# A macaron block on one core: the load queue written in block order, the scan's rows loaded twice, and z taken at the first place of a unit

## What is computed

```
x = x + 0.5 * ffn(layernorm(x))
x = x + attn(layernorm(x))
x = x + 0.5 * ffn(layernorm(x))

# attn: xz = x @ W_xproj.T -> delta_r (128), B (16), C (16)
delta = softplus(delta_r @ W_dt.T + b_dt)
dA = exp(delta * A);  Bu = delta * B * x          # 1024 channels x 16 states
h = dA * h + Bu                                   # over time
y = sum(h * C) + x * D_param
```

## Time and profile before

| | |
|---|---|
| median of 3 runs | 2799.12 us (2798.25 to 2800.99) |
| the profiled execution's own time | 2797.06 us |
| its span, first to last instruction | 2795.3 us |
| busy in the span | PE 2602.9, POOL 2348.2, DVE 2220.1, ACT 1496.2 us |
| mean granted PE clock | 0.985 |

### The profile page before, as it was taken

One profiled execution on the slowest core, in us unless ns is written; L12 is line 12 of the kernel. 1 busy time (PEld: TensorE's weight loads), 2 busy tenths in 40 slices (PEclk: granted clock), 3 DMA queues, 4 the chain that ended last, 5 costly groups with the idle time before them and its releaser, 6 DMA issues.

```text
span 2795.3 us, 39869 instructions
## 1 busy us (share of the span) xinstructions
PE 2602.9 (93%) x13664; PEld 1176.9 (42%) x13664; DVE 2220.1 (79%) x2933; ACT 1496.2 (54%) x3363; POOL 2348.2 (84%) x703
## 2 busy tenths in 40 slices
PE   4989999999999999999999999999999999989999
PEld 1444444444344443444444434444444443434444
DVE  8447888888888887888878888788888888888843
ACT  5346666665555655556555555565555554655521
POOL 2138889989899898998999989999899999989910
PEclk8999999999999999999999999999999999999999
DMA  5144544544354443644544445444455434454321
GB/s 219 48 116 137 144 127 131 161 142 139 109 164 140 135 138 112 163 140 127 147 143 132 144 137 163 138 126 129 151 153 158 143 119 141 136 145 145 91 58 53
DMA packets 303520, 373.50 MB, mean 134 GB/s; under 512 B 148435, under 2 KB 220243, under 8 KB 303318
## 3 DMA queue, kind: packets, MB, share of 16 engines
q1 hardware_dynamic: 286422, 337.40, 40.5%
q10 hardware_dynamic: 16896, 33.56, 4.1%
HBM read 234.05 MB, written 103.29 MB: 121 GB/s over the span
## 4 chain that ended last, share of the span: by engine, by line
PE 22%; DVE 19%; DVEq 5%; ACT 4%; DMA 4%; issue 4%; POOL 2%; SPq 1%; ACTq 1%; POOLq 0%
DVE mreg L1147 10%; PE pv L554 7%; PE po L554 5%; PE pv L558 3%; PE po L558 3%; PE py L721 2%; ACT pA L934 2%; DMA delta_scratch<-mreg 2%; DVE pv L1108 1%; DVE sel L1105 1%; DVEq L1113 1%; DMA mreg<-xnT_scratch 1%; DVEq L1107 1%; DVEq L1063 1%; DVE sel L1116 1%
## 5 line engine op out<-in xcount | busy, mean ns | idle before, releaser
L522 POOL TENSOR_TENSOR mreg<-mreg 128x2048 f32<-128x2048 f32 x256 | 1160.9, 4535 | 37.9 <-ACT hst L920 37.8
L1147 DVE TENSOR_TENSOR_SCAN mreg<-pA,hst,mreg 128x512 f32<-128x512 f32 (+1 forms) x1024 | 1042.9, 1065 | 98.9 <-ACT pA L934 70.0
L934 ACT ACTIVATE pA<-mreg,nA 128x512 f32<-128x512 f32 (+1 forms) x1280 | 739.0, 596 | 465.9 <-DVE mreg L1147 413.2
L512 POOL TENSOR_TENSOR mreg<-mreg 128x1024 f32<-128x1024 f32 x340 | 795.3, 2363 | 226.3 <-DMA mreg<-delta_scratch 219.6
L554 PE MATMUL pv<-wA,xT 128*128 128x512 f16 x2016 | 463.2, 382 | 40.5 <-DVE xT L1085 23.8
L554 PE MATMUL po<-wB,uT 128*128 128x512 f16 x2016 | 472.1, 381 | 13.5 <-DVE xin L1071 10.2
L554 PE MATMUL po<-wW,xT 128*128 128x512 f16 x2016 | 470.1, 380 | 0.0
L506 POOL TENSOR_TENSOR mreg<-mreg 128x2048 f32<-128x2048 f32 x86 | 389.7, 4532 | 1.4 <-issue 1.4
L554 PEld LDWEIGHTS pv<-wA,xT 128*128 128x128 f16 x2016 | 191.4, 98 | 323.1 <-ACT xT L841 60.3
L554 PEld LDWEIGHTS po<-wB,uT 128*128 128x128 f16 x2016 | 192.1, 98 | 277.9 <-issue 49.4
L554 PEld LDWEIGHTS po<-wW,xT 128*128 128x128 f16 x2016 | 196.0, 98 | 238.3 <-issue 24.6
(11 more groups left out here) (132 smaller groups left out, 2404.1 us busy)
## 6 DMA issues: line engine op xcount, KB each, us to landing
mreg<-delta_scratch SPq DMA_DIRECT2D x256, 512.0 KB, 6.0
delta_scratch<-mreg ACTq DMA_DIRECT2D x128, 256.0 KB
xin<-x SPq DMA_DIRECT2D x32, 512.0 KB, 3.7
x_scratch<-xin SPq DMA_DIRECT2D x32, 512.0 KB, 6.7
xnT_scratch<-auxs SPq DMA_DIRECT2D x32, 512.0 KB, 2.9
mreg<-xnT_scratch SPq DMA_DIRECT2D x64, 256.0 KB, 6.6
yT_scratch<-mreg SPq DMA_DIRECT2D x64, 256.0 KB, 2.5
uT<-yT_scratch SPq DMA_DIRECT2D x32, 512.0 KB, 4.7
```

Source lines behind the costliest of these rows:

```text
L512: pool.tensor_tensor(h[:, half * n:half * n + n, :], u, b.broadcast_to([P, n, c.width]), ALU.mult).then_inc(s_bm, 1)
L522: pool.tensor_tensor(h, h, by_c, ALU.mult).then_inc(s_cm, 1)
L934: last = nc.scalar.activation(dst[:, part, :], src[:, part, :], ACT.Exp, scale=nA[:, m:m + 1])
L1147: last = V.tensor_tensor_scan(h, split(pA[:, i % 2, :], c)[:, part, :], h, before, ALU.mult, ALU.add)
```

## The change

Four things change. **First**, SP's loads for the scan are no longer attached to groups (`slot`), but to blocks (`loads`): in each tile the first half of the next tile's inputs stands at place 6, the second at 7, the store of the tile before and the first delta pair at 9, the second delta pair at 15. A unit's blocks are listed in four parts: those of twentieths 0 to 2 at its head, 2 to 9 behind `turn`, 9 to 18 behind the stores of the rank rows, 18 to 20 behind the store of the unit's result. **Second**, a tile's rows of x are loaded twice: once for `delta` into one of two buffers that are free when `delta` has read them, and again at place 13 (`load_again`) into the third buffer, from which `sum_up` and the store work. **Third**, `plan` puts a tile's z at place 0 of the next unit that has none. A unit gets a second z, at place 1, only if the tile would otherwise come later than 10 groups before its own first group. **Fourth**, the load for the z at place 0 stands at the end of the unit before.

```
+AHEAD = 10
...
     for t in range(NTL):
-        s = 4 * t - 6
-        u, i = slot_unit[s] if s >= 0 else (SCAN0 - 1, 3)
-        at = (SCAN0 - 1, 2) if t == 0 else (u, 0) if i == 0 else (u, 1) if i < 3 else (u + 1, 0)
...
+        ready_at = f1_at[first_tile[t].row1 - 1] + 2 if t in first_tile else 0
+        late_u, late_i = slot_unit[max(4 * t - AHEAD, 0)]
+        at = (max(prev[0] + 1, ready_at), 0)
+        if at > (late_u + (late_i > 0), 0) and prev[1] == 0 and prev[0] >= ready_at:
+            at = (prev[0], 1)
...
             def load_tile(t):
                 sp.wait_ge(s_stn, 16 * chunk_of_tile[t].row1)
-                sp.wait_ge(s_sty[t % NXT], 16 * (t // NXT))
-                sp.dma_start(tile_of(t), blocks_of(xnT_u, t)).then_inc(s_ldt[t % NXT], 16)
+                sp.wait_ge(s_du, max(t - NXT + 2, 0))
+                slot = t % (NXT - 1)
+                sp.dma_start(tile_of(slot, t), blocks_of(xnT_u, t)).then_inc(s_ldt[slot], 16)
+
+            def load_again(t):
+                sp.wait_ge(s_sty, 16 * t)
+                sp.dma_start(tile_of(NXT - 1, t), blocks_of(xnT_u, t)).then_inc(s_ldv, 16)
...
-            def slot(a, n):
-                G = slot_of(a, n)
-                if G is None:
+            def loads(a, lo, hi):
+
+                if a.u < SCAN0 or a.u > SCAN1:
                     return
-                t = G // 4 + 1
-                if G % 4 == 2:
-                    if t >= 2:
-                        store_tile(t - 2)
-                    if t < NGRP // 4:
-                        spread_inputs(t, 0)
-                        spread_inputs(t, 1)
-                        spread_delta(t, 0)
-                if G % 4 == 3 and t < NGRP // 4:
-                    spread_delta(t, 1)
...
+                for i in range(block_at(a, lo), block_at(a, hi)):
+                    t, n = i // 16, i % 16
+                    if n == 6 and t + 1 < NTL:
+                        spread_inputs(t + 1, 0)
+                    if n == 7 and t + 1 < NTL:
+                        spread_inputs(t + 1, 1)
+                    if n == 9 and t >= 1:
+                        store_tile(t - 1)
+                    if n == 9 and t + 1 < NTL:
+                        spread_delta(t + 1, 0)
+                    if n == 13 and t < NTL:
+                        load_again(t)
+                    if n == 15 and t + 1 < NTL:
+                        spread_delta(t + 1, 1)
...
                 late = l if l and l.kind == 1 else None
-                if 0 not in a.zs:
-                    ranks_due(a, 1)
-                slot(a, 0)
-                if 0 in a.zs:
-                    load_tile(a.zs[0])
-                    ranks_due(a, 1)
+                ranks_due(a, 1)
+                loads(a, 0, 2)
...
                 turn(a, a.f2s + (b is not None and b.kind == 2))
-                slot(a, 1)
-                slot(a, 2)
                 if 1 in a.zs:
                     load_tile(a.zs[1])
+                loads(a, 2, 9)
...
-                slot(a, 3)
-                slot(a, 4)
-                if b:
-                    ranks_due(b, 0)
+                loads(a, 9, 18)
...
+                loads(a, 18, 20)
+                if b and 0 in b.zs:
+                    ranks_due(b, 0)
+                    load_tile(b.zs[0])
```

More of the change, by code:

```diff
@@ L95, in plan @@
     for t in range(NTL):
-        s = 4 * t - 6
-        u, i = slot_unit[s] if s >= 0 else (SCAN0 - 1, 3)
-        at = (SCAN0 - 1, 2) if t == 0 else (u, 0) if i == 0 else (u, 1) if i < 3 else (u + 1, 0)
[L99 to L102, removed]
+        ready_at = f1_at[first_tile[t].row1 - 1] + 2 if t in first_tile else 0
[3 more added lines that the diff above has]
+            at = (prev[0], 1)
+        if t == 0:
+            at = (SCAN0 - 1, 2)
+            assert f1_at[first_tile[0].row1 - 1] + 1 == at[0]
+        elif t > 2:
+            u, i = slot_unit[4 * t - 6]
+            assert at <= ((u, 0) if i == 0 else (u, 1) if i < 3 else (u + 1, 0)), (t, at)
         us[at[0]].zs[at[1]] = t
@@ L267, in build @@
         s_ldb = [sem(f"s_ldb{n}") for n in range(4)]; s_ldc = [sem(f"s_ldc{n}") for n in range(4)]
-        s_ldt = [sem(f"s_ldt{n}") for n in range(NXT)]; s_sty = [sem(f"s_sty{n}") for n in range(NXT)]
+        s_ldt = [sem(f"s_ldt{n}") for n in range(NXT - 1)]; s_ldv = sem("s_ldv"); s_sty = sem("s_sty")
         s_ldd = [sem(f"s_ldd{n}") for n in range(NPR)]; s_ldu = [sem(f"s_ldu{n}") for n in range(NPR)]
@@ L283, in column, with by_part @@
             return 16 * (channels_at(i // 16) + part) + i % 16
-        def rows_of(t):
-            return xt[:, t % NXT, :].rearrange("p (u k t) -> p k u t", k=chunk_of_tile[t].parts, t=P)
+        def by_part(slot, t):
+            return xt[:, slot, :].rearrange("p (u k t) -> p k u t", k=chunk_of_tile[t].parts, t=P)
         def split(a, c):
             return a.rearrange("p (k t) -> p k t", t=c.width)
-        def slot_of(a, n):
-            return a.slots[n] if n < len(a.slots) else None
         def block_at(a, twentieths):
@@ L331, in load_y @@
                     sp.wait_ge(s_out, a.u * 2 + 2)
-                    for n in range(NXT):
-                        sp.wait_ge(s_sty[n], 16 * len(range(n, chunk_of_row[b.v].tile1, NXT)))
+                    sp.wait_ge(s_sty, 16 * chunk_of_row[b.v].tile1)
                     src = yT_d[row:row + P, :].rearrange("p (k t) -> p k t", t=P)
@@ L382, in blocks_of, with tile_of @@
                 return d[:, c.row0:c.row1, k:k + c.parts, :].rearrange("p u k t -> p u (k t)")
-            def tile_of(t):
-                return xt[:, t % NXT, :].rearrange("p (u n) -> p u n", u=chunk_of_tile[t].rows)
+            def tile_of(slot, t):
+                return xt[:, slot, :].rearrange("p (u n) -> p u n", u=chunk_of_tile[t].rows)
             def load_tile(t):
                 sp.wait_ge(s_stn, 16 * chunk_of_tile[t].row1)
-                sp.wait_ge(s_sty[t % NXT], 16 * (t // NXT))
-                sp.dma_start(tile_of(t), blocks_of(xnT_u, t)).then_inc(s_ldt[t % NXT], 16)
+                sp.wait_ge(s_du, max(t - NXT + 2, 0))
[4 more added lines that the diff above has]
+                sp.dma_start(tile_of(NXT - 1, t), blocks_of(xnT_u, t)).then_inc(s_ldv, 16)
             def store_tile(t):
                 sp.wait_ge(s_y, t + 1)
-                sp.dma_start(blocks_of(yT_u, t), tile_of(t)).then_inc(s_sty[t % NXT], 16)
+                sp.dma_start(blocks_of(yT_u, t), tile_of(NXT - 1, t)).then_inc(s_sty, 16)
             def turn(a, y_done):
@@ L403, in turn @@
                     sp.dma_start_transpose(uT[:, part, :, :], src).then_inc(s_uc[part], 16)
-            def slot(a, n):
-                G = slot_of(a, n)
-                if G is None:
+            def loads(a, lo, hi):
+                if a.u < SCAN0 or a.u > SCAN1:
                     return
-                t = G // 4 + 1
-                if G % 4 == 2:
-                    if t >= 2:
-                        store_tile(t - 2)
-                    if t < NGRP // 4:
-                        spread_inputs(t, 0)
-                        spread_inputs(t, 1)
-                        spread_delta(t, 0)
-                if G % 4 == 3 and t < NGRP // 4:
-                    spread_delta(t, 1)
[L419 to L423, removed]
+                for i in range(block_at(a, lo), block_at(a, hi)):
[12 more added lines that the diff above has]
+                        spread_delta(t + 1, 1)
+                    for c in CH[1:]:
+                        if n % 4 == 0 and c.group0 - 4 <= i // 4 < c.group0:
+                            spread_b(c, i // 4 - c.group0 + 4)
+                        if n % 4 == 0 and c.group0 - 2 <= i // 4 < c.group0 + 2:
+                            spread_c(c, i // 4 - c.group0 + 2)
             def ranks_due(a, pos):
@@ L1129, in delta @@
                 dve.drain()
-                dve.wait_ge(s_ldt[t % NXT], 16 * (t // NXT + 1))
+                slot = t % (NXT - 1)
+                dve.wait_ge(s_ldt[slot], 16 * (t // (NXT - 1) + 1))
                 c = chunk_of_tile[t]
@@ L1133, in delta @@
                 V.tensor_tensor(dd[:, 1, :].rearrange(by_rows, k=c.parts, t=P), pz.rearrange(by_rows, k=c.parts, t=P),
-                                rows_of(t), ALU.mult).then_inc(s_du, 1)
+                                by_part(slot, t), ALU.mult).then_inc(s_du, 1)
             def scan(i):
@@ L1152, in sum_up @@
                 dve.wait_ge(s_e, 4 * t + 4)
+                dve.wait_ge(s_ldv, 16 * (t + 1))
                 c, k = chunk_of_tile[t], channels_at(t)
                 for n in range(c.parts):
-                    x_n = rows_of(t)[:, n, :, :]
+                    x_n = by_part(NXT - 1, t)[:, n, :, :]
                     y_n = split(py[:, :], c)[:, n, :].rearrange("p (u t) -> p u t", t=P)
```

## The result

The changed kernel takes **2819.5 us** (median of 4 runs, 2816.2 to 2822.1). The kernel before took 2800.05 us in the same comparison (2798.25 to 2803.07). The ratio is 1.007, with an interval of 1.0054 to 1.0086: slower by 0.7%, or 19.5 us, where 40 us less were forecast. The profiled execution took 2822.09 us, its span is 2820.3, and the mean granted clock is 0.982.

A forecast was written before the change was run, and what follows sets the result against it. PE and POOL were taken as nearly full, so what each waits for decides. Terms −73 − 7 + 37 + 3 = −40 us from 2797.06 gave 2757, forecast as 2760 us for the runs' median; range 2722 to 2798.

The forecast's parts named there:

- I take 0.65: Share of POOL's 112.3 us of input waits from `delta_scratch` expected to shorten the kernel: −73 us (bounds −30 and −112).
- length = POOL's work + POOL's idle: Ledger for stretches of eight units with the scan, such as 326.7 + 24.7 us; it set the gain's upper limit.
- comparison across rows 2: Units 24 to 31 against 40 to 47: 7.3 us more POOL idle, 9.5 us longer, so idle is paid in full.
- the waits change their names: Rival, chance 0.09: POOL waits for `hst` instead of inputs, only 0.27 of 112.3 us is won, 2802 us.
- So seven units at 5.3 us: Second delta pairs moved behind `turn` in units 10, 18, 26, 34, 42, 50, 58 come late: +37 us (+19 to +57).
- short stalls: Rival, chance 0.23: delta pairs land nearer 4 than 6.5 us, the seven cost 19 us, POOL's gain is 0.8; 2724 us.
- no slack between xn and PE: Unit 18: PE's `norm_blocks` started with no wait, so a late delta pair (5.7 us there) would delay PE.
- z at place 0: I take 0: 22 units move z ahead of the next unit's statistics; hidden by DVE's waits for PE, 0 us (31 us without cover).
- second z, −7: Units with two z: the earlier load of the tile's rows ends DVE's wait and PE's bank wait; −7 us (0 to −13).
- the second load at 0: 64 more loads of 256 KB for the tiles' rows, 16.8 MB, and their issues on SP: 0 us.
- The +3 for the ranks: Rank loads moved behind the result's store reach PE's z late ahead of unit 16: +3 us (0 to 5), once.
- the stalls outweigh: Rival, chance 0.13: late delta pairs hit units where PE had no wait; at 8.1 us each the sum is +23, 2822 us.

The follow-up runs named there:

- e9: e1 with both input halves moved from places 6 and 7 to place 9, behind the store of y: 2781.1 us.
- e1: The changed kernel with the second delta pair at place 12 instead of 15, for all tiles: 2759.1 us.
- e4: The kernel before with the double load of the rows and the new places of z, but the old queue by slots: 2781.1 us.
- e13: e1 with the place 0 z behind the next unit's statistics and norm on DVE and ACT, only in units with one z: 2740.9 us.
- e7: The changed kernel with the second delta pair at place 12 and z at the places of the kernel before: 2769.0 us.
- e3: The kernel before with only the double load of the tiles' rows added: 2798.5 us.
- e8: e1 with the second load of the rows at place 2 of the next tile instead of place 13: 2762.0 us.
- e6: The changed kernel with the second delta pair at place 12 only in units 10, 18, 26, 34, 42, 50 and 58: 2791.1 us.
- e15: The changed kernel with the second delta pair at place 15 only in units 10, 18, 26, 34, 42, 50 and 58, elsewhere at 12: 2789.2 us.

## Why the prediction was wrong

**"I take 0.65" of 112.3 us was the largest miss.** The waits ended, and with the pairs at place 12 that brought at most some 22 us (e9 to e1; e4 to e1, which is the whole of the queue's order, gives the same), not 73: a share of 0.2. The argument behind the share was the ledger "length = POOL's work + POOL's idle". It is true of any engine, bound or not, and so proves nothing about cause. The comparison across rows 2 (7.3 us more idle, 9.5 us longer) had the direction wrong: when another engine makes a unit longer, POOL's idle time grows with it. The kernel after shows it: its POOL is idle 198.5 us in units 3 to 59 against 174.7 before, without the input waits. The rival "the waits change their names" named the mechanism rightly, and its share of 0.27 was near. What decided was in the trace: PE waited for POOL 8.2 us in all, and for xn 36.7. That 8.2 is not the whole price either: in e9 PE's waits grow by some 14 us (10.7 for POOL, 3.0 for xn), its busy time at a lower clock by 5 (9 with the short records that are missing in e9's row), and the time by 22.

**"So seven units at 5.3 us" counted too few units.** In the seven the mechanism holds and the sum is smaller: 28 to 30 us (37 forecast), with ACT's wait, PE's behind it and the lower clock in unit 34 as described. The 5.3 us each do not hold. The pairs of the seven landed in 4.1 to 6.1 us and not in 6.5, as the rival "short stalls" had it, and in unit 18, "no slack between xn and PE" was wrong: of ACT's 3.78 us 1.29 reached PE. But the other tiles' pairs moved too, behind the unit's result (unit 4), or behind the rank stores (units 7 and 22), and against e1 that and units 9, 17 and 25 cost another 30 to 32. The prediction looked only at pairs that changed sides of `turn`.

Both misses show in one comparison without any experiment, by the starts of units: against the kernel before the seven grew by 26.0 us (37 forecast), and the other fifty of the stretch changed by −0.1 (−77 forecast, all the other terms). In e1 these fifty take 37 us less than before; place 15 gives all of it back.

**"z at place 0: I take 0"** was wrong as well. With z behind the statistics in 47 units the kernel gains another 18 us (e13); 22 units were moved, which by the same price is 18 x 22/47 = 8 us, an estimate. PE's wait for xn shows the same: 31.1 us with the old plan (e7), 51.6 with the new (e1). The plan as a whole still gains 10 to 17 us (e1 against e7, e4 against e3), so **"second z, −7"** was too small, though the waits that it named did end. How that gain divides among the units was not tried.

**Right were** the second load at 0 (e3, e8), the ends of the waits for `xnT_scratch` and the bank, and the growth of `hst` waits. The +3 for the ranks shows in no wait of PE's z.

The measured terms are 0 for the load, −17 for plan and second z, −22 for the queue with the pair at 12 and +60 for place 15, or +21 us in all against 19.5 measured. That they add up is no test, since e3, e4 and e1 are steps on one way from before to after; e6 against e15 and e9 are the tests. Of the rivals this is "the stalls outweigh", at 28 to 30 us in its seven units and as much again outside them. That its 2822 us lies so near the 2819.5 measured is luck: it had 57 us in the seven.

Order and landing act together outside the seven. Unit 4's pair went out 5 us later in unit 3 than in e1 and took 10.9 us to land where e1's took 5.4; unit 22's went out about 1 us later and took 10.1 for 8.5. What makes them land so slowly was not tried apart; e8, which takes the second load out of the way at place 12, gained nothing there.

## What to carry to other kernels

Price a wait by what the bound engine waits for, in its own rows, and not by how an engine's idle time goes with the length: that sum closes for every engine. The bound engine's rows give the order of the price and not all of it (8.2 us there, at most 22 measured). In a queue that issues in order, list for every moved transfer what it now stands behind in each unit, not in those that look worst: here three blocks for one 512 KB load were worth 60 of 2800 us. And when a change of several parts is slower, take its parts one by one before dropping it: one digit made it 1.5% faster than the kernel before, and an order of two steps 2.1%.

## What the runs showed of the hardware

A pair of the same 512 KB landed in 3.7 to 12.5 us in the kernel after, with a median of 6.0 (all loads of L354):

```profile
DMA to landing us min/median/max: 3.7/6.0/12.5
```

Before, the longest was 9.0 and the median 6.5: the tail grew, not the middle. The tail alone costs little: in e1 the same loads take 3.9 to 12.4 us (median 5.8), and ACT waits 8.2 us for them in all. Another 16.8 MB of loads, which raise the DMA share of the scan's stretch from 0.47 to 0.49 and its rate from 138 to 145 GB/s, cost no measurable time (e3).

With PE's gaps its clock falls, so they cost more than their length. Over units 3 to 59 its busy time for the same matmuls ran from 2331.8 us (e13, clock 1.00) to 2363.7 (after, 0.98), and its idle time from 108.2 to 159.4. Between these two, whose matmul records are of the same number, lie 83 us: 51 of idling and 32 of clock, 1.6 times the idling. The factor is not a constant: between e1 and the kernel before, also with records of the same number, 30.3 us of idling go with 8.0 of clock (1.3), between e9 and the kernel after 21.8 with 17.3 (1.8).
